# Spreading the first 256 stacked queries with products instead of transfers, in a one-core attention and expert kernel

## The reference, cut to what matters

```python
qkv = jnp.einsum('bsd,ed->bse', x, Wqkv_w) + Wqkv_b
q, k, v = ...                                  # 16 heads of 32; one k, one v of 32
scores = jnp.einsum('bqhd,bkd->bhqk', q, k) * scale      # causal
attn = jax.nn.softmax(scores, axis=-1)
out = jnp.einsum('bsd,ed->bse', ctx, out_w) + out_b
x = _layernorm(x + out)
x = _layernorm(x + experts(x))                 # top 2 of 8, silu(x1) * x3, bf16
```

## Time and profile before

| what | us |
|---|---|
| three runs | 1138.89, 1142.77, 1143.15; median 1142.77 |
| the profiled execution, its own time | 1142.1 |
| its span in the trace | 1140.3 |
| PE busy, share of the span | 1085.1, 95% |
| DVE busy | 881.0, 77% |
| ACT busy | 715.3, 63% |
| POOL busy | 192.4, 17% |
| mean granted clock of PE | 0.985 of full speed |

### The profile page before, as it was taken

How to read it: one execution, slowest core, us unless ns; L and a number is a source line. 1 busy time by engine, 2 the same in 40 slices (tenths; PEclk the granted TensorE clock), 3 DMA queues, 4 the chain that set the end, 5 groups by cost and what they waited for, 6 DMA issues and landing times.

```text
span 1140.3 us, 18344 instructions
## 1 busy us (share of the span) xinstructions
PE 1085.1 (95%) x6080; PEld 521.2 (46%) x6080; DVE 881.0 (77%) x1103; ACT 715.3 (63%) x844; POOL 192.4 (17%) x156
## 2 busy tenths in 40 slices
PE   6699999999999999999989999999999999999986
PEld 4246434743336543334734743474333654333442
DVE  3176799679985688988676669976998668898856
ACT  5344676558883488886436458744888437888721
POOL 2250223012112012111013013210211201211000
PEclk9799999999999999999999999999999999999988
DMA  4893430253001622000163254016400152200000
GB/s 139 220 168 77 117 74 9 72 126 92 1 1 39 149 75 38 1 1 18 46 153 86 65 121 112 2 40 146 112 1 1 39 119 68 38 1 1 2 1 37
DMA packets 41101, 74.36 MB, mean 65 GB/s; under 512 B 14224, under 2 KB 15248, under 8 KB 40976
## 3 DMA queue, kind: packets, MB, share of 16 engines
q1 hardware_dynamic: 25392, 58.74, 19.6%
q0 software_dynamic: 13584, 11.54, 6.8%
q10 hardware_dynamic: 2000, 2.51, 0.7%
HBM read 25.58 MB, written 8.39 MB: 30 GB/s over the span
## 4 chain that ended last, share of the span: by engine, by line
PE 83%; DVE 7%; issue 4%; ACT 2%; SPq 2%; POOL 2%; ACTq 0%; DMA 0%; DVEq 0%; POOLq 0%
PE sc L1109 22%; PE bank L1131 20%; PE sc L996 10%; PE sc L1249 9%; PE bank L996 7%; PE sc L1149 3%; DVE psum_k L793 3%; PE sc L1264 2%; SPq L393 2%; PE bank L1149 2%; PE bank L1264 2%; PE sc L1197 1%; PE bank L1257 1%; POOL prob L492 1%; ACT prob L620 1%
## 5 line engine op out<-in xcount | busy, mean ns | idle before, releaser
L620 ACT ACTIVATE prob<-sc 128x1024 f32<-128x1024 f32 x544 | 525.6, 1025 | 144.9 <-PE sc L1109 144.7
L793 DVE TENSOR_TENSOR psum_k<-psum_k,prob 128x2048 f32<-128x2048 f32 x170 | 403.5, 2373 | 4.7
L1109 PE MATMUL sc<-q_st,k_st 128*128 128x512 f32 x1088 | 329.4, 424 | 20.0 <-DMA q_st<-q_lo 8.7
L1109 PEld LDWEIGHTS sc<-q_st,k_st 128*128 128x128 f32 x1088 | 184.6, 189 | 262.9 <-ACT prob L620 177.7
L1131 PE MATMUL bank<-prob,v_sb 128*32 128x512 f32 x2176 | 287.4, 606 | 0.6 <-POOL prob L492 0.5
L492 POOL TENSOR_SCALAR_AFFINE_SELECT prob<-prob 128x1024 f32<-128x1024 f32 x64 | 112.2, 1793 | 539.8 <-ACT prob L620 539.8
L1249 PE MATMUL sc<-prob,w_sb 128*128 128x512 bf16 x512 | 120.8, 382 | 0.0
L1131 PEld LDWEIGHTS bank<-prob,v_sb 128*32 128x32 f32 x2176 | 44.4, 108 | 104.9 <-issue 87.4
L650 ACT ACTIVATE prob<-sc 128x512 f32<-128x512 f32 x64 | 38.0, 594 | 76.0 <-PE sc L1249 76.0
L996 PE MATMUL bank<-q_st,wq_hi 128*128 128x512 f32 x240 | 80.7, 401 | 0.0
L793 DVE TENSOR_TENSOR psum_k<-prob 128x2048 f32<-128x2048 f32 x28 | 64.0, 2287 | 19.8 <-POOL prob L492 15.8
(11 more groups left out here) (138 smaller groups left out, 996.0 us busy)
## 6 DMA issues: line engine op xcount, KB each, us to landing
q_st<-q_hi SPq DMA_DIRECT2D x128, 128.0 KB, 2.4
q_st<-q_lo SPq DMA_DIRECT2D x128, 128.0 KB, 2.4
res<-in_x SPq DMA_DIRECT2D x8, 1024.0 KB, 5.1
res<-ob_sb POOLq DMA_DIRECT2D x8, 1024.0 KB, 8.7
out_x<-res SPq DMA_DIRECT2D x32, 256.0 KB, 2.2
res<-in_xT SPq DMA_DIRECT2D x7, 1024.0 KB, 5.3
w_sb<-in_w POOLq DMA_DIRECT2D x8, 256.0 KB, 8.6
prob<-in_wqkvT ACTq DMA_DIRECT2D x4, 288.0 KB, 6.1
```

The lines of the kernel that those rows point to most:

```text
L620: nc.scalar.activation(prob[t % NP][:, half * HW:(half + 1) * HW], score_half(q // TB, 2 * t + half).rearrange("p m n -> p (m n)"), ACT.Ex ...
L793: nc.vector.tensor_tensor(acc[:, :], first[:, :], prob[t % NP][:, :], ALU.add).then_inc(add_v, 1)
L1109: last = nc.tensor.matmul(dst, k_st[:, k * P:(k + 1) * P], q_st[slot][:, c * HJ:(c + 1) * HJ, at:at + P], start=True, stop=not shift)
```

## The change

SP's `stack_queries(0, 0)` issues only half 1 (16 DMAs). Half 0 is made by PE: a selector `spread_sel` of ones and zeros (built by POOL, copied by ACT to PE's fast format) is multiplied with `q_hi` and then with `q_lo`, 32 rows each; the sum in the bank holds high, high, low, low of a row group c for two of its heads (n = 0 or 1) and 256 tokens. ACT copies six of the eight results to `q_st[0]`, DVE two. POOL waits for all eight and raises `stack_in[0][c]` by 64 each, in place of the transfers. The split input of the start moves from `q_st[0]` to `q_st[1]`. PE turns the identity 24 times before its first product. ACT's other work in the start is reordered: `pick` and the selector before the biases' wait, `gT` after the first squares, `ow_hi` in two halves after j = 1 and j = 2.

```diff
--- before.py
+++ after.py
@@ -52,6 +52,7 @@
 NP = 6
 LAG = 2
 HIGH_LAG, LOW_LAG = 4, 5
+WARM = 24
 BOUND = 60.0
 BOUND_KV = 1e9
 EARLY, LATE = range(5), range(5, E)
@@ -155,6 +156,7 @@
         mhalf = sb("mhalf", [P, TB])
         pick = sb("pick", [P, E], BF16)
         ident_b = sb("ident_b", [P, P], BF16)
+        spread_sel = sb("spread_sel", [P, 6 * HD], F32R)
 
         q_hi = sb("q_hi", [P, 2, HJ, PAIR], F32R)
         q_lo = sb("q_lo", [P, 2, HJ, PAIR], F32R)
@@ -199,6 +201,7 @@
         gT = sb("gT", [P, BT], BF16)
 
         pick_f = prob[1][:, 0:E]
+        spread_f = prob[1][:, P:P + 6 * HD]
         x1T = prob[0][:, :].rearrange("p (c t) -> p c t", c=DC)
         hT = psum_k[0][:, :].bitcast(BF16).rearrange("p (e t) -> p e t", e=E)
         silu = [prob[1][:, i * BT:(i + 1) * BT] for i in range(4)]
@@ -213,6 +216,9 @@
         xT_raw = [res[i][:, :, :].rearrange("p t d -> p (t d)").rearrange("p (c t) -> p c t", c=DC) for i in range(2)]
         stack_rows = q_st[0][:, :, :].rearrange("p h n -> p (h n)").rearrange("p (n c t) -> p n c t", n=2, c=DC)
         xT_hi, xT_lo = stack_rows[:, 0], stack_rows[:, 1]
+
+        start_rows = q_st[1][:, :, :].rearrange("p h n -> p (h n)").rearrange("p (n c t) -> p n c t", n=2, c=DC)
+        start_hi, start_lo = start_rows[:, 0], start_rows[:, 1]
 
         wq_raw = [prob[2 + c // 2][:, (c % 2) * (D + 2 * HD):(c % 2 + 1) * (D + 2 * HD)] for c in range(DC)]
         ow_raw = psum_k[0][:, :].rearrange("p (c e) -> p c e", c=DC)
@@ -241,6 +247,10 @@
         const_step = sem("const_step")
         consts_ready = sem("consts_ready")
         pick_ready = sem("pick_ready")
+        spread_ready = sem("spread_ready")
+        spread = sem("spread")
+        kept_by_act = sem("kept_by_act")
+        kept_by_dve = sem("kept_by_dve")
         rT_cleared = sem("rT_cleared")
 
         xT_in = sem("xT_in")
@@ -368,6 +378,12 @@
         def squares_bank(g):
             return LOW[5] if g == 0 else top[1]
 
+        def spread_bank(c):
+            return (LOW[2], LOW[3], LOW[4], top[0][:, :])[c]
+
+        def spread_heads(c, n):
+            return q_st[0][:, c * HJ + 2 * n:c * HJ + 2 * n + 2, :]
+
         def down_bank(g, t):
 
             return LOW[4 + t] if t < 2 else top[t - 2][:, :]
@@ -383,10 +399,10 @@
                 sp.dma_start(res[g % 2][:, :, :], x[seq, (g % NG) * BT:(g % NG + 1) * BT, :]
                              .rearrange("(t p) d -> p t d", p=P)).then_inc(res_in[g % 2], 16)
 
-            def stack_queries(b, g):
+            def stack_queries(b, g, halves=range(2)):
 
                 sp.wait_ge(low_out, count(b, low_out, 5 * (g + 1)))
-                for half in range(2):
+                for half in halves:
                     for c in range(HC):
                         for part in range(4):
                             src = (q_hi, q_hi, q_lo, q_lo)[part]
@@ -395,7 +411,7 @@
                                 src[c * HD:(c + 1) * HD, half, :, :].bitcast(F32),
                             ).then_inc(stack_in[half][c], 16)
 
-            stack_queries(0, 0)
+            stack_queries(0, 0, halves=[1])
             load_x(0, 0)
 
             with sp.Fori(0, B) as b:
@@ -454,6 +470,11 @@
                 step(nc.gpsimd.affine_select(out=pick_f, in_=pick_f, compare_op=ALU.not_equal,
                                              fill=1.0, base=-off, pattern=[[-1, E]],
                                              channel_multiplier=1))
+            step(nc.gpsimd.memset(spread_f, 0.0))
+            copies = spread_f.rearrange("p (a k) -> p a k", a=3)[:, 0::2, :].rearrange("p a (n m) -> p a n m", n=2)
+            for c in range(HC):
+                step(nc.gpsimd.affine_select(out=copies, in_=copies, compare_op=ALU.not_equal, fill=1.0,
+                                             base=-c * HD, pattern=[[0, 2], [0, 2], [-1, HD]], channel_multiplier=1))
             step(nc.gpsimd.memset(ident_b[:, :], 0.0))
             step(nc.gpsimd.affine_select(out=ident_b[:, :], in_=ident_b[:, :], compare_op=ALU.not_equal, fill=1.0,
                                          base=0, pattern=[[-1, P]], channel_multiplier=1))
@@ -478,6 +499,10 @@
                                              fill=1.0, base=-c * HD, pattern=[[-1, E]], channel_multiplier=1))
             nc.gpsimd.memset(rden[:, :], 0.0).then_inc(consts_ready, 1)
 
+            pool.wait_ge(kept_by_act, 6)
+            pool.wait_ge(kept_by_dve, 2)
+            for c in range(HC):
+                pool.sem_inc(stack_in[0][c], 64)
             pool.wait_ge(weights_in, 3 * 16)
             pool.wait_ge(ow_low, 1)
 
@@ -550,10 +575,13 @@
             for c in range(DC):
                 act.wait_ge(first_in[c], 2 * 16)
                 nc.scalar.activation(wq_hi[:, c, :], wq_raw[c], ACT.Copy).then_inc(first_high, 1)
-                nc.scalar.activation(xT_hi[:, c, :], xT_raw[0][:, c, :], ACT.Copy).then_inc(first_high, 1)
+                nc.scalar.activation(start_hi[:, c, :], xT_raw[0][:, c, :], ACT.Copy).then_inc(first_high, 1)
             act.dma_start(rT_sb[:, :, 0:E], rT.rearrange("(c p) e -> p c e", p=P)).then_inc(weights_in, 16)
             act.dma_start(ob_sb[:, :], ob.rearrange("(a n) -> a n", a=1).broadcast_to([P, D])).then_inc(weights_in, 16)
             act.dma_start(ow_raw, owT.rearrange("(c p) e -> p c e", p=P)).then_inc(weights_in, 16)
+            act.wait_ge(const_step, 6 + 5)
+            nc.scalar.activation(pick[:, :], pick_f, ACT.Copy).then_inc(pick_ready, 1)
+            nc.scalar.activation(spread_sel[:, :], spread_f, ACT.Copy).then_inc(spread_ready, 1)
             act.wait_ge(biases_in, 2 * 16)
 
             def split_high_k(b, g):
@@ -592,15 +620,19 @@
             split_high_q(0, 0, 0)
             square_kv(0, 0)
             square_q(0, 0, 0)
+            act.wait_ge(consts_ready, 1)
+            nc.scalar.activation(gT[:, :], rden[:, :], ACT.Copy).then_inc(pick_ready, 1)
             for j in range(1, HJ):
                 split_high_q(0, 0, j)
                 square_q(0, 0, j)
-            act.wait_ge(weights_in, 3 * 16)
-            nc.scalar.activation(ow_hi[:, :, :], ow_raw, ACT.Copy).then_inc(ow_high, 1)
-            act.wait_ge(consts_ready, 1)
-            act.wait_ge(const_step, 6 + 1)
-            nc.scalar.activation(pick[:, :], pick_f, ACT.Copy).then_inc(pick_ready, 1)
-            nc.scalar.activation(gT[:, :], rden[:, :], ACT.Copy).then_inc(pick_ready, 1)
+                if j < HJ - 1:
+                    part = slice((j - 1) * DC // 2, j * DC // 2)
+                    act.wait_ge(weights_in, 3 * 16)
+                    nc.scalar.activation(ow_hi[:, part, :], ow_raw[:, part, :], ACT.Copy).then_inc(ow_high, 1)
+            for n, c in ((0, 0), (0, 1), (1, 0), (1, 1), (1, 2), (1, 3)):
+                act.wait_ge(spread, HC * n + c + 1)
+                nc.scalar.activation(spread_heads(c, n), spread_bank(c).rearrange("p (j t) -> p j t", j=2),
+                                     ACT.Copy).then_inc(kept_by_act, 1)
             act.wait_ge(pick_ready, 2)
 
             with act.Fori(0, B) as b:
@@ -689,7 +721,7 @@
                 nc.vector.tensor_tensor(wq_lo[:, c, :], wq_raw[c], wq_hi[:, c, :].bitcast(F32),
                                         ALU.subtract).then_inc(first_low, 1)
                 dve.wait_ge(first_high, 2 * c + 2)
-                nc.vector.tensor_tensor(xT_lo[:, c, :], xT_raw[0][:, c, :], xT_hi[:, c, :].bitcast(F32),
+                nc.vector.tensor_tensor(start_lo[:, c, :], xT_raw[0][:, c, :], start_hi[:, c, :].bitcast(F32),
                                         ALU.subtract).then_inc(first_low, 1)
             dve.wait_ge(consts_ready, 1)
             dve.wait_ge(biases_in, 2 * 16)
@@ -759,10 +791,14 @@
             keep_v(0, 0)
             split_low_q(0, 0, 2)
             split_low_q(0, 0, 3)
+            for c in (2, 3):
+                dve.wait_ge(spread, c + 1)
+                nc.vector.tensor_copy(spread_heads(c, 0), spread_bank(c).rearrange("p (j t) -> p j t", j=2)
+                                      ).then_inc(kept_by_dve, 1)
             fold_norms(0, 0)
             top_of_norms(0, 0)
             judge(0, 0)
-            dve.wait_ge(ow_high, 1)
+            dve.wait_ge(ow_high, 2)
             nc.vector.tensor_tensor(ow_lo[:, :, :], ow_raw, ow_hi[:, :, :].bitcast(F32),
                                     ALU.subtract).then_inc(ow_low, 1)
 
@@ -1045,22 +1081,47 @@
                 last.then_inc(normed, 1)
 
 
+            def spread_queries(c, n):
+
+                if n == 0:
+                    pe.wait_ge(low_out, 3)
+                else:
+                    pe.wait_ge(low_out, 5)
+                    if c < 2:
+                        pe.wait_ge(kept_by_act, c + 1)
+                    else:
+                        pe.wait_ge(kept_by_dve, c - 1)
+                rows = slice(c * HD, (c + 1) * HD)
+                nc.tensor.matmul(spread_bank(c), spread_sel[rows, 0:P], q_hi[rows, 0, 2 * n:2 * n + 2, :],
```

(17 more changed lines are left out.)

## The result

| | us |
|---|---|
| before, 5 runs | 1141.54 (1138.89 to 1143.15) |
| after, 5 runs | 1130.14 (1128.01 to 1133.34) |
| ratio | 0.9904, 95% interval 0.9879 to 0.9928 |
| forecast | 1128.8, range 1125.0 to 1133.5 |
| spans of the profiled executions | 1140.3 before, 1126.9 after |

The kernel is 1.0% faster, 11.4 us between the medians; the forecast had 14.0. In the changed kernel L409 is the stack's DMA, L399 the residual's load, L1170 the scores, L1032 the split products, L1102 the turns of the identity, L1095 and L1097 the spreading, L634 and L796 its copies.

A forecast was written before the change was run, and what follows sets the result against it. It took the start to be bound by SP's issue rate, and the part behind by PE. Profiled 1142.1 - 13.5 = 1128.6 us; with the three-run median 0.7 above, it said 1128.8, range 1125 to 1133.5.

The forecast's parts named there:

- the stretch of the 32 DMAs: Start of group 0, 25.43 to 48.56 us: only SP's stack transfers on the chain, one issued every 0.64 us.
- the residual's path: From the residual's load through POOL's bias and masks to PE's bank: 13.2 us, ending last, with a PE stall of 1 us.
- The first DMA: SP's first stack transfer, after the last low split: forecast at 23.65 us instead of 25.41, 1.76 us earlier.
- load_x: The residual's load on SP's queue: forecast 10.25 us behind the last low split, at 33.9 us instead of 46.73.
- rival 1: At the start, turns don't raise PE's clock; first products stay 0.43 us apart; gain 11.7, 1130.4 us; chance 35%.
- the two terms that were too small: At the start: the last low split done at 23.65 us, and the residual's load issued 10.25 us behind it.
- the turns don't lift the clock: The claim of rival 1, at PE's start: the last low split stays at 25.43 us, time 1130.4 us; chance 35%.
- The slower rival: PE stays at 1.2 GHz through group 0's attention: 25.5 - 13.5 = +12 us, 1154 us; chance 3%.
- the 25.5 us of work: PE's products in group 0's attention (10 tiles and denominators), which would take twice as long at the lower clock.
- A part bound by SP's issue rate: Start of group 0: SP issues one stack DMA every 0.64 us; behind it a part bound by PE.
- The verdict: The scores' other condition, ending with no_shift: forecast at 28.0 us, setting the first scores at 29.35 instead of 30.86.
- the copies: End of the spreading: ACT's last copy forecast at 28.4 us, the stack ready by 28.7, 0.65 us sooner than needed.

The follow-up runs named there:

- run 1: The changed kernel again, unedited, as a control: median 1129.80 us, ratio 0.9905 to the kernel before.
- run 7: Changed kernel with POOL's masks ahead of the residual's bias (1132.67 us), 22 added turns (1132.60), both (1137.25), or both with 2 starting turns instead of 24 (1134.07).
- run 5: The kernel before with each of the 32 stack transfers cut in two, 64 of 64 KB: 1163.08 us, ratio 1.0188.
- run 4: The kernel before with eight of the 32 stack transfers issued from ACT's queue instead of SP's: 1139.74 us, ratio 0.9985.
- run 2: The changed kernel without the 24 turns of the identity: 1132.55 us, ratio 0.9913 to the kernel before.

## Why the prediction was right

**That the stretch of the 32 DMAs was the place, and that all behind it moves: right.** The turns of x1 moved by 11.8 us in the profile and 12.8 in run 1's.

**That the residual's path is late next: right, term by term.** Forecast 13.2 from load_x to the eighth tile; 13.1 in the profile, 12.9 to 13.2 in the six traces in which it ended last. Moving the masks took it off the chain (run 7). The forecast had PE stall 1.0 us; it was 0.71.

**The size: 2.6 us too large, of which the terms explain most.** 1.2 of the 2.6 lie in the kernel before: the forecast started from the median of three runs, 1142.77, and five have 1141.54. The first DMA was put at 23.65 and went at 24.28 (the third chunk was late; 23.78 in run 1). load_x was put 10.25 behind it and went 11.25 behind (10.3 to 11.25 in the traces that issue the 16 alone): I had taken the faster of the two sixteens of the earlier trace rows, the slower had 11.06, with the slow issue beside a block of instructions in it (run 1). These two make 1.6 of the 13.5, and the profile has 12.0. Run 1's trace has 13.0. The medians' 11.4 lie below both, as far as a scatter of 4 us tells.

**What was luck.** The landmarks of the changed kernel's trace are nearer to rival 1's numbers than to the forecast's own: load_x at 35.53 (rival 35.7, forecast 33.9), the eighth tile at 48.64 (48.9, 47.1), the median 1130.14 (1130.4, 1128.8). By the time alone the rival would have fitted as well. Only the start of the trace tells them apart, and the two terms that were too small happened to add up to nearly what the rival takes away (1.6 and 1.8 us).

**The rivals.** That the turns don't lift the clock, which the Trainium skill's "TensorE: Matmul & The Clock Gate" (Part 4) would have, is refuted by this trace, for 24 turns of 128x128 in fp32: the turns go from 0.21 to 0.11 us apart at 5.2, and the products stand 0.23 us apart at 7.85, against 0.43 without turns. The 1.8 us that it would have cost are of the size that SP's issues vary by. The slower rival, the low clock through group 0, came in part: ten microseconds instead of none, and they lay beside the residual's path. The clock fell at 26, before the stretch for which I had thought of it, and was back at 36, ahead of most of the 25.5 us of work.

**Where the reason was incomplete.** "A part bound by SP's issue rate" holds for one queue: each DMA took 0.63 us there, the same for half the bytes (run 5). But a second limit lies right behind it, at 0.65 us for each DMA of 128 KB (run 4). The sum wasn't touched, since the change takes DMAs away; a plan to share them out over two queues, drawn from the same sentence, would have gained nothing.

**Two terms that didn't matter.** The verdict was put at 28.0 and ended at 28.79 (sums 0.5 us late, norms turned at the lower clock), the copies at 28.4 and ended at 29.63: so the spreading, not the verdict, released the first scores, at 30.17 instead of 29.35 (28.96 in run 1). Leaving it out brought them to 29.45 and moved nothing behind in this stretch.

## What to carry to other kernels

Count the DMAs on the path as well as their bytes: here each took 0.63 us of its queue with 128 KB and with 64, and a second queue didn't help at 128, so taking them away (a product with ones and zeros, on an engine that idles there) was the way. When a stretch is cut by more than 10 us, follow every transfer that was issued behind it to its last reader: the end of this gain was set by a residual's load that PE didn't wait for in the kernel before. And read a gain of 1 us in the trace at the end of the kernel too: edits that shortened the start by 1 to 2 us gave that back, and up to 3 us a sequence more, in places that they didn't touch.

## What the runs showed of the hardware

- Turns of the identity alone raise TensorE's clock: 24 turns from 1.73 us, 0.21 us apart at first and 0.11 from 5.2 us on, then products 0.23 us apart at 7.85; without them 0.43 (run 2). 22 more turns in PE's idle times held it at 1.00 from 25 to 37 us in one trace; in another with the same turns it was 0.50 from 28 to 30 (run 7).
- A DMA of 64 or 128 KB within on-chip memory takes 0.63 us of its queue when one queue issues. With two queues six were issued in 1.9 us, and the 32 of 128 KB still landed one each 0.65 us (runs 4 and 5).
- An issue now and then takes 1.2 to 1.6 us instead of 0.59, and in these traces it overlaps a 16 KB block of instructions on q8 (run 1).
- Products of 32 rows in four row groups run at once: eight of 512 columns in 0.74 us.
- PE has idle times with no semaphore behind them, often about the last denominators of a group, of 0.34 to 2.65 us in group 0. In group 0 they end 2.57 to 2.67 us behind the start of a 16 KB block of instructions, in twelve of twelve traces (run 7). They depend on the kernel's code ahead of the loop (22 instructions more: 2 to 3 us in the fourth group of both sequences) and, in group 1, differ between two executions of one kernel (117.7 and 118.8 us for the step).
- The last group's routing can spend more or less time at the lower clock: 42.5 us from the last turns of x1 to the end in the trace of before, where the clock was 0.50 for the first 8 us, 40.1 after, where it was back within 4, and 40.1 to 42.8 in the other kernels. These 2.4 us are more than the 1.6 by which the spans (13.4 us apart) differ beyond 11.8.
